# Residual transformer stack with two expert layers on one core: VectorE's side work of the second attention block moved between the head pairs, and two expert weight loads issued before the routing tables

## The reference

```python
x = x + L0_xcond(layernorm(x), cond, ctx)   # self attention, cross attention over ctx, gated feed forward
x = x + L0_ffn(layernorm(x))                # 64 experts, the best 8 of each token, and a shared one
x = x + L1_xcond(ctx, layernorm(x), ...)    # 112 queries attend to 375 context rows and themselves, 16 heads
x = x + L1_ffn(layernorm(x))                # 8 experts, the best one of each token

# L1_xcond, for each of the 16 sequences
kv_in = concat(layer_norm(ctx), lat)        # 375 + 112 = 487 keys
q, k, v = lat @ Wq.T, split(kv_in @ Wkv.T)  # 16 heads of 64
out = (softmax(q k^T / 8) v) @ Wo.T

# L1_ffn, for each token
idx = argmax(x @ Wr + br); gate = softmax(x @ Wr + br)[idx]
out = gate * (gelu(x @ W1[idx] + b1[idx]) @ W2[idx] + b2[idx])
```

## Time and profile before

| | |
|---|---|
| median of 3 runs | 3069.35 us (3068.98 to 3071.95) |
| the profiled execution, its own time | 3071.95 us |
| its span, first to last instruction | 3070.2 us |
| PE busy | 2818.3 us, 92% |
| DVE busy | 1519.8 us, 50% |
| ACT busy | 1047.8 us, 34% |
| POOL busy | 908.8 us, 30% |
| chain that ended last: PE | 85% of the span |
| chain that ended last: DVE | 5% of the span |
| one round of the third stage | 62.3 us ((2127.52 - 1940.61) / 3, starts of three rounds apart) |

### The profile page before, as it was taken

How to read it: one execution, slowest core, us unless ns; L and a number is a source line. 1 busy time by engine, 2 the same in 40 slices (tenths; PEclk the granted TensorE clock), 3 DMA queues, 4 the chain that set the end, 5 groups by cost and what they waited for, 6 DMA issues and landing times.

```text
span 3070.2 us, 58371 instructions
## 1 busy us (share of the span) xinstructions
PE 2818.3 (92%) x17275; PEld 1936.9 (63%) x17276; DVE 1519.8 (50%) x4412; ACT 1047.8 (34%) x2721; POOL 908.8 (30%) x1782
## 2 busy tenths in 40 slices
PE   7999999999999999995999948999999999999795
PEld 5776666666776666664788724555555555556464
DVE  4445555544545555544655524455555555554332
ACT  1333333333333333332343313344333433343121
POOL 1012222122112222112555533443344344430211
PEclk9999999999999999997999979999999999999898
DMA  6000000000000000002588850100001000100331
GB/s 214 8 6 7 7 7 7 7 7 2 7 5 7 7 7 7 7 2 97 154 268 256 176 149 18 30 26 18 18 19 35 20 18 18 35 3 2 136 142 60
DMA packets 89263, 154.74 MB, mean 50 GB/s; under 512 B 16964, under 2 KB 64720, under 8 KB 87664
## 3 DMA queue, kind: packets, MB, share of 16 engines
q1 hardware_dynamic: 39760, 85.60, 8.5%
q0 software_dynamic: 21072, 42.53, 6.1%
q10 hardware_dynamic: 28368, 25.83, 2.5%
HBM read 121.93 MB, written 31.98 MB: 50 GB/s over the span
## 4 chain that ended last, share of the span: by engine, by line
PE 85%; DVE 5%; issue 4%; DMA 2%; ACT 1%; POOL 1%; DVEq 0%; ACTq 0%; POOLq 0%
PE psG L895 14%; PE psG L889 12%; PE psG L883 12%; PE psG L905 8%; PE psT L856 7%; PE psO L869 6%; PE psG L841 6%; PE psG L1220 4%; PE psG L1297 2%; PE psO L1312 2%; PE psO L1232 2%; DMA kT<-normed_rows,ids 1%; PE psT L796 1%; PE psG L1211 1%; DVE nmax L1792 1%
## 5 line engine op out<-in xcount | busy, mean ns | idle before, releaser
L895 PE MATMUL psG<-W,ctxT 128*125 128x512 f32 (+2 forms) x896 | 403.9, 596 | 0.0
L1440 ACT ACTIVATE probs<-psG,nmax 112x375 f32<-112x375 f32 (+1 forms) x512 | 316.7, 620 | 239.8 <-DVE nmax L1792 239.8
L889 PE MATMUL psG<-ctxT,W 128*128 128x375 f32 (+1 forms) x1024 | 392.5, 531 | 1.1 <-ACT ctxT L1627 1.1
L1792 DVE TENSOR_REDUCE nmax<-psG 112x1 f32<-112x375 f32 (+1 forms) x512 | 285.2, 601 | 150.5 <-PE psG L841 150.4
L883 PE MATMUL psG<-hT,W 128*128 128x112 f32 x2560 | 308.4, 279 | 18.7 <-ACT hT L1465 17.7
L856 PEld LDWEIGHTS psT<-ident,probs 112*125 112x125 f32 (+2 forms) x1792 | 203.4, 167 | 191.0 <-ACT probs L1440 146.2
L883 PEld LDWEIGHTS psG<-hT,W 128*128 128x128 f32 x2560 | 295.6, 194 | 35.6 <-ACT hT L1465 26.9
L889 PEld LDWEIGHTS psG<-ctxT,W 128*128 128x128 f32 x1024 | 190.0, 190 | 166.4 <-issue 115.0
L856 PE MATMUL psT<-ident,probs 112*125 112x112 f32 (+2 forms) x1792 | 255.9, 279 | 32.1 <-ACT probs L1440 23.8
L895 PEld LDWEIGHTS psG<-W,ctxT 128*125 128x125 f32 (+2 forms) x896 | 160.5, 186 | 180.7 <-issue 178.8
L841 PE MATMUL psG<-kT,qT 64*112 64x375 f32 (+1 forms) x1024 | 250.4, 566 | 11.3 <-ACT ctxT L1627 10.7
(11 more groups left out here) (348 smaller groups left out, 4108.6 us busy)
## 6 DMA issues: line engine op xcount, KB each, us to landing
expert_rows<-kT ACTq DMA_DIRECT2D x197, 128.0 KB, 1.8
W<-in_ew SPq DMA_DIRECT2D x64, 384.0 KB, 4.5
W<-in_ew SPq DMA_DIRECT2D x8, 2048.0 KB, 8.9
ctxT<-in_ctxT SPq DMA_DIRECT2D x16, 375.0 KB, 3.2
kT<-in_ctx SPq DMA_DIRECT2D x16, 375.0 KB
W<-in_eb SPq DMA_DIRECT2D x8, 640.0 KB, 10.2
normed_rows<-hrow SPq DMA_DIRECT2D x32, 112.0 KB, 1.9
kT<-normed_rows,ids POOLq DMA_INDIRECT x197, 4.0
```

The lines of the kernel that those rows point to most:

```text
L889: mm = nc.tensor.matmul(bank[:, 0:n], wt[:, c, n0 + j * P:n0 + (j + 1) * P], src[:, c, 0:n], start=(c == 0), stop=(c == DC - 1))
L895: mm = nc.tensor.matmul(bank[0:kn, 0:512], src[:, c, k0:k0 + kn], wt[:, c, n0 + half * 512:n0 + (half + 1) * 512], start=(c == 0), stop=(c ...
L1440: nc.scalar.activation(probs[:, 2 * (s % 2) + i, 0:keys], psG[0:T, score_banks(s)[i], 0:keys], ACT.Exp, bias=nmax[:, h:h + 1], accum_out=r ...
L1792: nc.vector.tensor_reduce(nmax[:, 2 * s + i:2 * s + i + 1], psG[0:T, score_banks(s)[i], 0:keys], AXX, ALU.max, negate=True).then_inc(max_r ...
```

## The change

On DVE's side:

- `context_piece` is gone; `ahead` now returns a function of the step, and `attention` calls it twice after each pair. Steps 0 to 7 carry the eight adds of batch b+2, step 8 `measure_latents`, step 9 the whole of `measure_context`, steps 10 to 17 the eight parts of `compact` for batch b+3. Steps 16 and 17 lie after the last copy of the probabilities and ahead of `invert_sums`.
- `slots1` of a batch no longer stands at the end of the round in which its ranks are made; its two halves stand at steps 0 and 1 of the next attention (from batch 2 on). The last one is run in `tables1`, behind `x3_done`.
- `keysL` and the first value copy carry nothing any more. The loop begins at batch 2 instead of 1.

On SP's side, `experts1` issues the weights of experts 2 and 3 as soon as `x3_done` is there. Before, that stood behind `xT_full`, the transposes of the first block.

```diff
@@ experts1 (SP) @@
-                for e in range(2):
-                    arrived1(e)
-                sp.wait_ge(s.xT_full, 1)
                 weights1(2)
                 weights1(3)
-                for e in range(2, 4):
+                for e in range(4):
                     arrived1(e)
                 sp.wait_ge(s.tables, 1)
@@ tables1 (DVE) @@
+                slots1(B - 2, 0)
+                slots1(B - 2, 1)
                 tile_T1(B - 1)
@@ DVE @@
-            def context_piece(b, s):
-
-                if s in (4, 6, 8):
-                    if s == 4:
-                        dve.wait_ge(ctxr_in, 16 * b + 16)
-                    c = (s - 4) // 2
-                    note(nc.vector.bn_stats(cst[0:SC, c, :], ctxr[:, c, :]))
-                if s == 10:
-                    settled()
-                    for c in range(NS):
-                        e = nc.vector.bn_aggr(cmv[0:SC, c, :], cst[0:SC, c, :])
-                    e.then_inc(ctx_stats, 1)
-
-            def ahead(b, more, i):
-
-                if i < 2:
-                    for k in range(4 * i, 4 * i + 4):
-                        add_rows(b, k)
-                if i == 2:
-                    measure_latents(b)
-                if more and i >= 2:
-                    for k in range(3 * i - 6, min(3 * i - 3, 8)):
-                        compact(b + 1, k)
+            def ahead(b, more, r=None):
+
+                def at(s):
+                    if r is not None and s < 2:
+                        slots1(r, s)
+                    if b is None:
+                        return
+                    if s < L0E.K:
+                        add_rows(b, s)
+                    if s == L0E.K:
+                        measure_latents(b)
+                    if s == L0E.K + 1:
+                        measure_context(b)
+                    if more and s >= L0E.K + 2:
+                        compact(b + 1, s - L0E.K - 2)
+                return at
 
-            def keysL(behind=None):
+            def keysL():
                 for j in range(1, IC, 2):
                     bank = filled()
                     nc.vector.tensor_copy(kT2[:, j, :], bank[:, 0:KV]).then_inc(dve_evac, 1)
-                    if behind:
-                        behind(j // 2)
 
-            def batchL(b, more, more2, more3, turned=True):
-                attention(KV, KC, spreadL, (lambda s: context_piece(b + 2, s)) if more2 else None)
+            def batchL(b, more, more2, more3, turned=True, routed=True):
+                attention(KV, KC, spreadL, ahead(b + 2 if more2 else None, more3, b - 2 if routed else None))
                 jobs.skip()
                 if more:
-                    behind = (lambda i: ahead(b + 2, more3, i)) if more2 else None
-                    keysL(behind)
+                    keysL()
                     valuesL(0)
-                    if behind:
-                        behind(4)
...
                 if turned:
                     places1(b - 1)
-                    slots1(b - 1, 0)
-                    slots1(b - 1, 1)
-
-            batchL(0, True, True, True, False)
-            with dve.Fori(1, B - 3) as b:
-                jobs.enter(b - 1, DVEL_JOBS)
-                unit.enter(b - 1, 16)
-                step.enter(b - 1, 28)
-                halves.enter(b - 1, 2)
+
+            batchL(0, True, True, True, False, False)
+            batchL(1, True, True, True, True, False)
+            with dve.Fori(2, B - 3) as b:
+                jobs.enter(b - 2, DVEL_JOBS)
+                unit.enter(b - 2, 16)
+                step.enter(b - 2, 26)
+                halves.enter(b - 2, 2)
                 batchL(b, True, True, True)
             for t in (jobs, unit, step, halves):
-                t.leave(B - 4)
+                t.leave(B - 5)
```

## The result

The changed kernel takes 3120.68 us (median of 4 runs, 3115.72 to 3121.62), the kernel before 3069.73 beside it (4 runs, 3068.98 to 3071.95): a ratio of 1.0161, interval 1.0148 to 1.0172, so 51 us slower. All 21 executions of the changed kernel on record lie between 3111.76 and 3123.15. 3119 was forecast. The profiled execution of the changed kernel took 3111.76 us with a span of 3110.0, 9 less than its median. Single executions differ by some us in stages that no change here touches: in the 13 traces of this document the third stage's first attention starts between 1871.4 and 1878.1 us. So what follows is read from lengths inside the third stage and the passage behind it, not from spans.

What follows compares the result with a forecast made beforehand. PE was taken to bound the third stage, DVE's side work costing only where PE waits for it. 28.6 + 2.1 + 1.4 - 0.8 + 11.9 + 6.5 = 49.7 us more gave 3119 us, range 3105 to 3126.

Steps and rivals of the forecast that it cites:

- The round: Each loop round, batches 2 to 12, loses 0.7 at the start, 0.7 at pair 5, 1.2 at the end: 2.6 us.
- at the copies of pair 7: Late in each attention, DVE's lateness adds some 0.2 us at pair 7, within the end's 1.2.
- Pairs 1 to 3 cost nothing: With two adds per pair DVE's period is 2.80 us, just below PE's 2.86, so PE waits for nothing: cost 0.
- rival 2: DVE becomes the bound of pairs 0 to 4: 3.5 us a round, 10 more in all, 3129 us; chance 0.12.
- Rival 1: Pairs absorb a late maximum, only single events count: round near 0, 3083 us; chance 0.12 together with rival 4.
- rival 4: SP's stream alone decides: passage takes 10 us more, attentions as in Rival 1, 3087 us; chance 0.12 together with Rival 1.
- Batches 1, 13, 14 and 15: Attentions outside the loop: batch 1 loses 2.1 us, batch 13 1.4; batches 14 and 15 gain 0.4 each at the start.
- The first attention: Its first add waits for batch 2's gather: 6.9 us late, 3.5 for the clock, 1.5 for the rest; 11.9.
- The clock: After PE's pause in the first attention, some 7 us of work at half speed, costing 3.5 us.
- The rest of this round: What else the first attention's round loses, beyond the late transposes and the clock: 1.5 us.
- The passage: Weights beside the scatters and table gather before the last stage: 2 + 3 + 1.5, 6.5 us more.
- Rival 3: The change is faster: `slots1` gone from the first maximum gains 0.48 us 12 times, 5.8, giving 3064; chance 0.04.

Runs made afterwards that it cites:

- e1: The kernel before with only SP's part of the change, weights of experts 2 and 3 issued at `x3_done`: 3077.22 us, ratio 1.0031.
- e2: The changed kernel with SP's part undone, DVE's part alone: 3107.53 us, ratio 1.0137 to the kernel before.
- e3: The changed kernel with the last two parts of `compact` moved from steps 16 and 17 to behind the first value copy: 3103.27 us, ratio 1.0118.
- e6: The changed kernel with `measure_context` split, statistics at steps 9, 11 and 13, aggregates at 15: 3106.67 us, ratio 1.0136.
- e11: The changed kernel with one extra statistic of 0.42 us on constant rows at steps 3, 5 and 7: 3128.0 us, ratio 1.0205.
- e9: The changed kernel with `slots1` back at the end of the round, adds still at steps 0 and 1: 3112.77 us, ratio 1.0154.
- e10: The changed kernel with batch 0's side work as before: context pieces between the pairs, the steps in groups behind the key copies: 3104.34 us, ratio 1.0133.
- e7: The kernel before with `slots1` at steps 2 and 3 of the next attention and the loop beginning at batch 2: 3060.61 us, ratio 0.9983.

## Why the prediction was right, step by step

**That waits of PE for DVE are the cost, and where.** Right. The four waits named are there (1.16 at pair 1, 0.87 at L793, 7.2 in the first attention), the one at pair 5 with 0.32 where 0.7 was named, and `e1` and `e2` show that the parts add.

**The round.** 2.6 forecast, 2.34 measured. Taken from the first score matmul: the transposes of pair 1 stand at 6.04 (5.89 forecast, 5.30 before), those of pair 5 at 18.05 (18.05 forecast, 16.74 by before's period), those of pair 7 at 23.20 (21.70 before), L793 at 26.18 (23.83). Put to the places as the prediction has them, with the late second half of the transposes (1.18 us long instead of 1.00) at its own pair, the costs are 0.92 at pair 1, 0.57 at pair 5, nothing at pair 7 and 0.85 at the end, against 0.7, 0.7, 0.2 and 1.0. The mechanism was right in three of the four. The 0.2 "at the copies of pair 7" was wrong: that wait was there before the change. Pair 1 was too low by 0.2: the maximum came at 4.03 and not at 3.88, and the second half costs 0.18. So part of the good agreement is errors that cancel. Over 11 rounds the term is 25.4 where 28.6 was forecast. `e3` prices the end at 0.88, `e6` pair 5 at 0.58.

**Pairs 1 to 3 cost nothing.** Right, by little: DVE's period is 2.77 where 2.80 was worked out, and `e11` shows what rival 2 would have been (3.1, and 1.07 per round). Rival 1, that the pairs absorb a late maximum, falls with the wait of 1.16 at pair 1 and with `e11`. Of rival 4 the half on the stream came true (9.8 in `e1`, 10 said), and the half that it takes from rival 1 did not.

**Batches 1, 13, 14 and 15.** 1.6 against 2.1 and 0.95 against 1.4, both for the term of pair 5: DVE is less late there, and the step at pair 5 is 0.23 and 0.24, not 0.7. For the last two -0.8 was forecast and +0.5 measured. The step that failed is "batches 14 and 15 only gain at the start". PE's first transposes of batch 14 start 2.85 behind the first score matmul before the change and 2.68 after it, a gain of 0.17 where 0.4 was put, and those of batch 15 gain nothing (2.68 and 2.67). Between pairs 0 and 1, `slots1` pushes the transposes of pair 1 in batch 14 from 4.95 to 5.11, and in both batches their second half comes some 0.2 late. `e9`, with `slots1` in the old place, has them at 4.78 and gives 0.73 back in these two batches. It also has the first transposes of batch 14 at 2.68, so even the 0.17 can't be put down to `slots1`; what it comes from is open.

**The first attention.** 11.9 forecast, 9.6 measured; `e10` shows that it all comes from the side work in this attention, and the timeline that 8.6 of it is there by pair 2. The gather's landing was right: the add starts 10.10 us behind the first score matmul, 10.08 forecast, and pair 1's transposes come 6.74 later than before, 6.9 forecast. The clock was mis-sized, 3.5 against at most 1.9 (pair 2's transposes are 8.62 late, the second half's wait included). I read the price of the earlier trace rows for a pause of PE of 9.5 us. Here PE stood 7.2, with the granted clock at 1.00 until 1880; it is 0.50 from 1884 to 1888, where PE works again, and 0.92 on the mean of 1888 to 1892. The work at 0.50 (1.2 GHz) is some 4 us by these means, not 7. "The rest of this round", 1.5, was 1.0.

**The passage.** 6.5 forecast, 8.6 measured in this trace (9.8 in `e1`; the nine kernels with the stream at `x3_done` have 25.8 to 28.0, the three without it 17.6 to 18.2). The scatters took 9.9 and 6.6 beside the weights, 5.4 and 2.2 before: 4.5 and 4.4 more, where I took 2 and 3. The table gather paid nothing here, where I took 1.5: it was issued at 2897.89 and landed in 2.7, while the stream moved only 0.03 MB from 2898 to 2899. In `e1` it paid 1.8. So the two scatters are the terms that were mis-sized.

The rule of the Trainium skill (DMA: Bandwidth & Descriptors, Queues, rings and completion order), that an engine changes between its queues at the end of a packet, would give about 3 by the prediction's estimate, whose price of a packet isn't shown; the scatters' rows don't bear that size out. The first scatter, the second one and the token gathers each lost 3.9 to 5.8 us beside this stream. What in the DMA engines makes it so was not tried.

**Rival 3** (faster by the 0.48 alone) is real as a mechanism, as `e7` shows, and lost to what was put in the same place.

The misses partly cancel: the terms of the attentions are 43.2 against 38.0, the passage 6.5 against 8.6. The total of 49.7 against the medians' 51 is closer than its terms, 49.7 against 46.6 placed, and that nearness is luck. The table gather was issued 8.9 us later than before, and not "some 5".

## What to carry to other kernels

An engine that is half idle can have no room where it counts: the gap between two waits of the bounding engine is the budget, to be counted per iteration from starts in the timeline, side operation by side operation, with the waits between dependent ones. Work moved from a phase in which the bounding engine never waits into one in which it waits for that engine can only gain if it fits those gaps, and an operation that waits for a transfer must not be moved ahead of its landing. Prefetching large weights ahead of their need can have a price where small dependent transfers run at the same time: here 8.6 us in the passage.

## What the runs showed of the hardware that was not expected

A scatter of 112 rows of one word landed 9.9 and 6.6 us after its issue beside 5.4 MB of weights, 5.5 and 2.2 us without them; a gather of token rows 7.3 instead of 2.8. The second scatter of the changed kernel landed at 2897.1, some 3 us ahead of the stream's last piece, which landed 20.2 after its issue at 2880.2. So it did not have to wait for the stream's end; how the two share the DMA engines is open.

After a pause of 7.2 us the lower granted clock cost at most 1.9 us; the score matmuls of the first attention ran at 0.50 before the change as well, behind their own pause of 9.5 us.

The same four small operations of `slots1`, at the end of a round, put off PE's first transposes of the next attention by 0.48 us in the register loop (3.10 and 2.62 behind the first score matmul), by 0.17 ahead of batch 13, the first behind the loop (2.79 in `e9`, 2.62 in the changed kernel), and not at all ahead of batches 14 and 15 (`e9` against the changed kernel). Why is open.
